# One output group moved across a block boundary, and vector work re-dealt in the second stage of a two-stage block kernel

## The reference

```python
h = layernorm(x) * (1 + ca) + sa
# mixer
qkv = rms(h) @ w_qkv.T;  q, k, v = split(qkv);  q, k = rms(q), rms(k)
w = exp(k)
y = sigmoid(q) * (cumsum(w * v) / (cumsum(w) + 1e-6))      # along the tokens
u, g = split(y @ w_swiglu.T)                                # 2048 each
x = x + ga * (h + (u * silu(g)) @ w_out.T)
# feed-forward, 4-bit weights with a scale for each group of 128 inputs
h = layernorm(x) * (1 + cb) + sb
gate, up = split(h @ dequant(gate_up).T)                    # 1408 each
y = (silu(gate) * up) @ dequant(down).T
x = x + gb * y / rms(y)
```

## Time and profile before

| | us |
|---|---|
| median of three runs | 2029.94 (2029.45 to 2031.5) |
| the profiled execution's own time | 2029.91 |
| its span in the profile | 2027.9 |
| PE busy | 1881.1 (93%) |
| DVE / ACT / POOL busy | 1427.0 / 924.6 / 871.1 |
| first swiglu step starts at | 175.2 |
| feed-forward starts at | 1418.0 |

### The profile page before, as it was taken

How to read it: one execution, slowest core, us unless ns; L and a number is a source line. 1 busy time by engine, 2 the same in 40 slices (tenths; PEclk the granted TensorE clock), 3 DMA queues, 4 the chain that set the end, 5 groups by cost and what they waited for, 6 DMA issues and landing times. The chain is left out here.

```text
span 2027.9 us, 25283 instructions
## 1 busy us (share of the span) xinstructions
PE 1881.1 (93%) x8376; PEld 825.8 (41%) x8376; DVE 1427.0 (70%) x1805; ACT 924.6 (46%) x1421; POOL 871.1 (43%) x616
## 2 busy tenths in 40 slices
PE   4738999999999999999999999999999999999797
PEld 1213444444444444444444444444444343344242
DVE  6997687876877686786787675425657757767756
ACT  4435334424423523533442441221666676676574
POOL 0554324423523432432442331221676766767564
PEclk7869999999999999999999999999999999999999
DMA  7223012112021021010211101203301011101011
GB/s 297 81 79 124 27 39 67 59 39 66 10 83 63 17 83 53 28 61 26 66 59 38 46 22 53 79 16 113 137 22 63 4 60 63 35 28 42 0 42 63
DMA packets 66881, 119.38 MB, mean 59 GB/s; under 512 B 4720, under 2 KB 28272, under 8 KB 65264
## 3 DMA queue, kind: packets, MB, share of 16 engines
q1 hardware_dynamic: 66800, 118.40, 17.2%
HBM read 80.11 MB, written 38.27 MB: 58 GB/s over the span
## 5 line engine op out<-in xcount | busy, mean ns | idle before, releaser
L597 PE MATMUL bank<-Y,wsw 128*128 128x512 f16 x3072 | 682.8, 379 | 0.8 <-DVE late L960 0.8
L597 PEld LDWEIGHTS bank<-Y,wsw 128*128 128x128 f16 x3072 | 300.5, 98 | 365.8 <-issue 4.2
L900 POOL TENSOR_TENSOR late<-late 128x512 f16<-128x512 f32 x128 | 181.5, 1418 | 611.1 <-ACT late L750 610.3
L1772 DVE SCALAR_TENSOR_TENSOR f_A<-bank,gu_s,f_A 128x512 f32<-128x512 f32 x352 | 258.6, 741 | 181.8 <-ACT f_A L1605 174.8
L574 PE MATMUL bank<-late,wout 128*128 128x512 f16 x1536 | 352.4, 379 | 4.3 <-POOL late L900 4.3
L1679 POOL TENSOR_TENSOR f_A<-f_A 128x512 f32<-128x512 f32 x176 | 262.0, 1489 | 167.9 <-DVE f_A L1772 167.9
L1605 ACT ACTIVATE f_A<-bank,gu_s 128x512 f32<-128x512 f32 x352 | 240.4, 686 | 163.4 <-PE bank L1537 141.1
L550 PE MATMUL bank<-H,wqkv 128*128 128x512 f16 x1152 | 261.0, 385 | 41.2 <-DVE H L985 30.9
L1501 PE MATMUL bank<-f_HH,f_down_hi 128*128 128x512 f16 x704 | 266.3, 380 | 11.4 <-POOL f_HH L1691 10.4
L960 DVE TENSOR_TENSOR late<-late,bank 128x512 f32<-128x512 f32 x128 | 87.4, 683 | 252.6 <-PE bank L597 248.9
L574 PEld LDWEIGHTS bank<-late,wout 128*128 128x128 f16 x1536 | 149.7, 98 | 194.3 <-issue 19.7
(11 more groups left out here) (160 smaller groups left out, 2075.7 us busy)
## 6 DMA issues: line engine op xcount, KB each, us to landing
X<-xT SPq DMA_DIRECT2D x15, 1024.0 KB, 5.6
room<-packed SPq DMA_DIRECT2D x48, 176.0 KB, 2.4
h_scratch<-X SPq DMA_DIRECT2D x8, 1024.0 KB, 4.4
f_X<-x_scratch SPq DMA_DIRECT2D x8, 1024.0 KB, 5.4
x_scratch<-X SPq DMA_DIRECT2D x28, 256.0 KB, 2.1
h_scratch<-SQ SPq DMA_DIRECT2D x28, 256.0 KB, 2.2
outT<-f_X SPq DMA_DIRECT2D x7, 1024.0 KB, 4.2
wout<-wmodT SPq DMA_DIRECT2D x1, 4096.0 KB, 14.3
```

The costliest lines, as they stand in the source:

```text
L597: mm = nc.tensor.matmul(out[:], wsw[:, pw, k, col:col + P], Y[:, px, k, :], start=(k == 0 and pw == 0 and px == 0), stop=(k == DT - 1 and ...
L900: nc.gpsimd.tensor_tensor(UG[:, j % 2, 1, :], G, UG[:, j % 2, 0, :], ALU.subtract).then_inc(UG_low, 1)
L1772: nc.vector.scalar_tensor_tensor(a, EV[ev_bank(j, m, steps)][:], gu_s[:, which * I_T + j, g:g + 1], a, ALU.mult, ALU.add).then_inc(by_dve, 1)
```

## The change

In the mixer, `output(b, 15)` of blocks 0 to 5 is taken from the end of the block and put behind group 0 of the `qkv` that follows. `n_squares` and `n_sqrt` each stand one copy later. `s1_split` stands ahead of `high(14)`, and `s1_low` at step 14.

In the feed-forward, two of ACT's takes (step 5, m = 4 and 6) in blocks 1 to 7 are done by DVE (`open_tile`), with a semaphore of their own. `add_y` goes from places 14, 17, 20 to 15, 16, 19. `result` goes from DVE to POOL, at places 31, 35, 39 and 43, behind POOL's `low` and ahead of its `half(j, 1)`. The last block's results in the tail stay on DVE.

```diff
@@ qkv (TensorE)
                         n += 1
+                        if not (isinstance(b, int) and b <= 1) and n == 1:
+                            output(b - 2, FT - 1)
@@ swiglu (TensorE)
-                output(b, FT - 1)
+                if not s1:
+                    output(b, FT - 1)
@@ s2_copies (ScalarE)
-                    if n == DT and not (isinstance(b, int) and b == 1):
+                    if n == DT + 1 and not (isinstance(b, int) and b == 1):
                         n_squares(b - 2)
-                    if n == 2 * DT + 1 and not (isinstance(b, int) and b == 1):
+                    if n == 2 * DT + 2 and not (isinstance(b, int) and b == 1):
                         n_sqrt(b - 2)
@@ iteration (ScalarE)
-                    high(b, j)
                     if s1 and j == 14:
                         s1_split(b + 2)
+                    high(b, j)
@@ iteration (VectorE)
-                        if j == 15:
+                        if j == 14:
                             s1_low(n)
@@ ffn
-        ADD_Y = {14: 0, 17: 1, 20: 2}
+        ADD_Y = {15: 0, 16: 1, 19: 2}
-        RESULT = {35: 0, 36: 1, 38: 2, 39: 3}
+        RESULT = {31: 0, 35: 1, 39: 2, 43: 3}
+        OPENS = [(Y_MEAN // DT, 4), (Y_MEAN // DT, 6)]
@@ beside (GpSimd)
+                if prev and place in RESULT:
+                    result(b - 1, RESULT[place])
@@ iteration (ScalarE)
-                        take(b, j, m, steps)
+                        if not by_vector(b, j, m):
+                            take(b, j, m, steps)
@@ VectorE
+            def open_tile(b, j, m, steps):
+                which, g = m // DT, m % DT
+                dve.wait_ge(group_done, GROUPS * (I_T * b + j) + m + 1)
+                nc.vector.tensor_scalar(A[:, slot(j), 2 * which + g // 2, :], EV[ev_bank(j, m, steps)][:],
+                                        gu_s[:, which * I_T + j, g:g + 1], None, ALU.mult).then_inc(opened_dve, 1)
...
+                        if by_vector(b, j, m - 1):
+                            open_tile(b, j, m - 1, steps)
                         take(b, j, m, steps)
```

More of the change, by code:

```diff
@@ L1355, in ffn @@
         scaled, H_high, H_low = map(sem, ("scaled", "H_high", "H_low"))
-        group_done, by_act, by_dve = map(sem, ("group_done", "by_act", "by_dve"))
+        group_done, by_act, by_dve, opened_dve = map(sem, ("group_done", "by_act", "by_dve", "opened_dve"))
         halves, gate_silu, hid_ready = map(sem, ("halves", "gate_silu", "hid_ready"))
@@ L1399, in ffn, with by_vector, opened @@
         NORM_Y = {30: 0, 31: 1, 32: 2, 34: 3}
-        RESULT = {35: 0, 36: 1, 38: 2, 39: 3}
-        assert RESULT.keys().isdisjoint(NORM_Y.keys())
+        RESULT = {31: 0, 35: 1, 39: 2, 43: 3}
+        OPENS = [(Y_MEAN // DT, 4), (Y_MEAN // DT, 6)]
+        def by_vector(b, j, m):
+            return not first(b) and (j, m) in OPENS
+        def opened(b, j, m):
+            if by_vector(b, j, m):
+                return opened_dve, len(OPENS) * (b - 1) + OPENS.index((j, m)) + 1
+            if first(b):
+                return by_act, DT * j + m // 2 + 1
+            skipped = sum(1 for o in OPENS if o < (j, m))
+            return by_act, (DT * I_T - len(OPENS)) * b + len(OPENS) + DT * j + m // 2 + 1 - skipped
         def now(place, start, step=1):
@@ L1467, in sums_left @@
                 pe.wait_ge(by_dve, DT * (I_T * b + steps.start))
-                pe.wait_ge(by_act, DT * (I_T * b + steps.start))
+                pe.wait_ge(*opened(b, steps.start - 1, GROUPS - 2))
             def mean(b):
@@ L1532, in iteration @@
                             back, k = last
-                            pe.wait_ge((by_act, by_dve)[k % 2], DT * (I_T * b + j - back) + k // 2 + 1)
+                            if k % 2:
+                                pe.wait_ge(by_dve, DT * (I_T * b + j - back) + k // 2 + 1)
+                            elif j < back:
+                                pe.wait_ge(*opened(b - 1, I_T - 1, k))
+                            else:
+                                pe.wait_ge(*opened(b, j - back, k))
                         which, g = m // DT, m % DT
@@ L1553, in _ @@
             pe.wait_ge(by_dve, DT * I_T * NB)
-            pe.wait_ge(by_act, DT * I_T * NB)
+            pe.wait_ge(*opened(NB - 1, I_T - 1, GROUPS - 2))
             for c in range(DT):
@@ L1687, in add_y, with result @@
                 nc.gpsimd.tensor_tensor(RSY[:], RSY[:] if n else SQY[:, 0, :], SQY[:, n + 1, :], ALU.add).then_inc(y_sum, 1)
+            def result(b, c):
+                pool.wait_ge(res_loaded, 16 * (b + 1))
+                pool.wait_ge(y_norm, DT * b + c + 1)
+                nc.gpsimd.tensor_tensor(X[:, c, :], X[:, c, :], Y[:, c, :], ALU.add).then_inc(out_ready, 1)
             def low(b, j):
@@ L1769, in take @@
                 dve.wait_ge(group_done, GROUPS * (I_T * b + j) + m + 1)
-                dve.wait_ge(by_act, DT * (I_T * b + j) + m // 2 + 1)
+                dve.wait_ge(*opened(b, j, m - 1))
                 a = A[:, slot(j), 2 * which + g // 2, :]
@@ L1785, in beside @@
                         work(c)
-                for places, work in ((INVERT_Y, invert_y), (NORM_Y, norm_y), (RESULT, result)):
+                for places, work in ((INVERT_Y, invert_y), (NORM_Y, norm_y)):
                     if prev and place in places:
```

## The result

The changed kernel takes 2010.67 us (median of four runs, 2008.06 to 2010.89), beside 2029.7 for the kernel before on the same chip: a ratio of 0.9902 [0.9885, 0.992], so 19 us faster. The forecast was 2012.3, with a range of 2001 to 2021. The profiled execution took 2010.48, its span is 2008.7, 19.2 shorter than the 2027.9 before.

The account below looks back on a forecast made before the run. PE was taken to bound the kernel, busy 1881.1 of 2027.9 us. Mixer 4.8, ordinary feed-forward blocks 10.2, block 6 3.7 and tail -1.1 sum to 17.6 us, giving 2012.3 from 2029.91; range 2001 to 2021, for 8 in 10.

Parts of the forecast that it names:

- Mixer, the stalls removed: In each mixer block, three PE waits of 0.72, 1.38 and 1.04 us go, 3.14 in all.
- rival 4: Words for `decode_chunk` load late behind the residual's stores, delaying copies PE needs; slower, 2036 at 4 us beyond room; chance 0.04.
- Mixer, what comes back: The DVE chain behind `n_sqrt` makes PE wait in `swiglu`, so each of five loop blocks gains 0.62 us, not 3.14.
- rival 1: The DVE chain behind `n_sqrt` does not bind, so the mixer gives 19.2 us: 1998; chance 0.12.
- The last `qkv`: At the mixer's last `qkv`, the gain is the room `hidden(0)` had before, 1.7 us.
- Ordinary feed-forward blocks: Blocks 1 to 5 and 7: fewer waits for POOL and ACT gain 1.7 us each, 10.2 for six.
- The contention: Feed-forward places 30 to 41: `norm_y` and POOL's results wait for each other, costing 1.25 us instead of 1.05.
- rival 2: POOL's results contend with DVE at all four feed-forward places: 0.7 us a block instead of 1.7, 2020.8; chance 0.14.
- Block 6: Feed-forward block 6: norm's root 2.5 us earlier, plus 1.2 for results leaving the DVE chain: 3.7 us gained.
- rival 3: DVE misses instructions at each of the mixer's four loop jumps, so 12.5 us come back: 2024.8; chance 0.04.
- Tail: At the end, the fourth result ahead of `half(10, 1)` makes the last chain later: -1.1 us.
- the forecast's own bounds: Whole kernel: a mixer gain of 0 to 8 us and ordinary blocks of 1.0 to 2.3 each give 2005 to 2019.

## Why the prediction was right, step by step

**Mixer, the stalls removed: right.** All three went, 3.14 us a block; group 0 found H ready, and PE has no wait inside `qkv` that late words of `decode_chunk` would have caused (rival 4 falls).

**Mixer, what comes back: right in mechanism and size.** Forecast was a gain of 0.62 for each block from a chain behind `n_sqrt` that takes most of the 3.14 back. Measured is a period shorter by 0.47 (164.65 to 164.18, forecast 164.0). The chain's links hold: 9.70 us from the reciprocal to `hidden(0)` (forecast 9.56), and 9.10 to the end of `hidden(1)` where 9.09 was forecast. One link was missing. I let PE reach G of step 1 at its own pace and put the first wait at U(1), on `hidden(0)`. In the trace PE waits 1.77 already at G(1), for `silu(0)`, which on ACT stands behind `n_split` and so behind the same DVE chain. The 0.2 us ahead of `hidden(0)`, which I had read as a wait for PE, is there again with DVE's own reciprocal named for it. The wait at G(1) costs little more, because U(1) comes 2.59 behind G(1) and would have waited for `hidden(0)` anyhow: that G, U pair is 5.54 long instead of 5.35, so both conditions end within 0.2 us of each other. The experiment with the root moved back proves the chain, and refutes rival 1 (nothing comes back).

**The last `qkv`: right.** Forecast was 1.7 for it. PE's second sum for the K norm comes once a block, ahead of the new waits, and marks the blocks: between these marks the intervals were 167.54, four times 164.65 and 165.02, and are 162.90 and five times 164.17. The first gained 4.64, 1.5 more than the three stalls, because waits in block 0's own `swiglu` fell away too (before 0.90 for POOL's sum and 0.53 for its low part). That is not the edit's doing. The kernels with the same mixer as the changed one have these waits in five profiles (0.91 to 1.68, and 0.53), among them the mixer's edits alone, and lack them in one (without `OPENS`, which runs at the lower clock there for a while); their first interval is 164.63 to 165.42, not 162.90. With the mixer of before it was 167.54 and 168.42. So the edit is worth about 3 in the first interval, what the stalls cost, and the rest is scatter between executions. The four gained 0.48 each, the last 0.85, and behind the last mark 1.76 came back. The total, 5.6, is thus 1.5 of scatter, 5 x 0.47, and about 1.8 for the last `qkv`. Without the scatter it is 4.1, and the forecast's 4.8 has 0.7 too much in the five blocks.

**Ordinary feed-forward blocks: right.** 1.85 to 2.06 each, forecast 1.7. The wait of 0.93 went; place 24 waits 0.83 for `low(4)` (forecast 0.8); place 36 costs 0.57 (0.85), and place 34 0.16 (0.4). The contention was over-sized: `norm_y` of place 32 took 1.10 us beside the first result, not 1.76, and that result, which also lay beside the end of `norm_y` of place 31, 1.72 instead of the 1.26 of the others. DVE's two `norm_y`, then POOL's results:

```profile
1596.96 0.98 DVE L1783 SCALAR_TENSOR_TENSOR f_Y<-f_Y,mod,f_RY 128x512 f32<-128x512 f32 x1
...
1598.53 1.10 DVE L1783 SCALAR_TENSOR_TENSOR f_Y<-f_Y,mod,f_RY 128x512 f32<-128x512 f32 x1
```
```profile
1597.36 1.72 POOL L1715 TENSOR_TENSOR f_X<-f_X,f_Y 128x512 f32<-128x512 f32 x1
...
1604.20 1.27 POOL L1715 TENSOR_TENSOR f_X<-f_X,f_Y 128x512 f32<-128x512 f32 x1
```

At the other three places DVE had only takes from a bank, and neither engine was slowed; rival 2 falls. By the three kernels that take a part back, `add_y` is worth 1.1 and `OPENS` 0.7; the results' move is worth 0.1 (69.32 to 69.34 against 69.40 to 69.42, block 1 69.49 against 69.57).

**Block 6: 3.7 forecast, 1.98 measured; the missing term is the clock.** The norm's root comes 1.85 us earlier in the block (49.12 to 47.27 into it), not 2.5. The 1.2 for the results leaving the DVE chain did come. The two waits that I had counted for them, 1.25 at place 38 and 0.40 at place 40 in the kernel before, are gone, and they are back in the two kernels that have the results on DVE, but for the first where a spell covers it. Behind the root's wait the block takes 40.83 before and 40.84 with the results on DVE; with three of them on POOL 39.57, and with all four and `add_y` back 39.17, neither with a spell at the lower clock. That is 1.3 and 1.7 less, with 0.6 paid for contention at place 33 already in it (a wait of 0.93 where it was 0.30). The changed kernel takes 40.70 there, because its spell at place 36 costs 1.5. So 1.85 + 1.66 - 1.53 = 1.98. The kernel before paid nothing for its own spell. My forecast had no term for the clock, though the column in the earlier trace rows said 0.98 for this block.

**The loop's edge at block 4: not in the sum.** I used only to imagine such edges in the mixer (rival 3, which did not come). In the feed-forward the results' move sent the 1 MB load from 0.5 us ahead of the jump to 6.4 behind it, worth 2.15 beyond the ordinary gain. With the 1.7 in block 6, which the spell hid, it is what the results' move brought: ordinary blocks would have had their gain without it.

**Tail: wrong in size, -1.1 forecast.** The fourth result delays `half(10, 1)` as I put it, by about 0.9 us of wait. In this execution the longer wait was followed by the lower clock, which added 1.7:

```profile
1987.93 0.38 PE L1518 MATMUL bank<-f_HH,f_down_hi 128*128 128x512 f16 x1 [2.39 <-POOL f_HH L1719]
...
1989.43 1.06 PE L1518 MATMUL bank<-f_HH,f_down_hi 128*128 128x512 f16 x2
```

From the last down projection's first matmul to the norm's sum are 5.21 us, before 3.53. With the fourth result on DVE the wait is 1.46 and the pair takes 0.59:

```profile
1987.70 0.38 PE L1519 MATMUL bank<-f_HH,f_down_hi 128*128 128x512 f16 x1 [1.46 <-POOL f_HH L1720]
1988.13 0.59 PE L1519 MATMUL bank<-f_HH,f_down_hi 128*128 128x512 f16 x2
```

So -2.6 instead of -1.1, of which -0.9 is the mechanism that I had forecast and -1.7 the clock. The kernel with `n_lower` later has the changed kernel's feed-forward and the same wait of 2.39, and no spell: 3.53 us from there to the norm's sum, and block 7 with the tail takes 94.3 instead of 96.0, 1.2 less than before where I had forecast 0.6 less.

The total came within 1.6 us because the misses cancel, and that is luck: mixer +0.8, ordinary blocks and block 7 +1.4, prologue +0.4, loop's edge +2.2, against -1.7 in block 6 and -1.5 in the tail. The plus of the mixer comes from the scatter of its first block, and the 0.44 of the prologue is scatter too: over the thirteen profiles the first `swiglu` step starts between 172.3 and 175.2, in kernels that do not differ there. Both big minuses are spells at the lower clock. The range that I gave for the forecast's own bounds, 2005 to 2019, was also too narrow by its own terms: a mixer of 0 with ordinary blocks of 1.0 makes 2021.

**Do the spells come in every execution?** Four kernels share the changed kernel's feed-forward: itself, the feed-forward's edits alone, the root one copy earlier, and `n_lower` later. In block 6 all four have the spell at the same place (87.97 to 87.99). In the tail three have it and one has not. The three kernels with three results on POOL share a feed-forward as well, and have no spell, one and two in block 6 (86.50, 86.46 and 87.61). So the same instructions and the same waits come with and without it, and it moves a single time by 1 to 2 us. What decides it stays open. Open too is which instructions come late at the jump, and for which engine.

## What to carry to other kernels

When stalls are removed ahead of a chain on another engine, ask when that chain's head is due on the new clock: here the head was moved one step later to cure a stall of 1.04 us, and the chain behind it cost 2.74. Follow every queue that hangs on the chain, not only the engine at its end: ACT's `silu` stood behind a split that waited for the same tiles. When work is moved between engines, follow the DMAs that its completion releases, and where they land against a loop's jump. And before a stretch of one trace is compared with another's, look at its granted clock: a spell hid 1.5 us of gain in block 6 here and cost nothing in the kernel it was compared with.

## What the runs showed of the hardware

- **A hardware loop's jump.** After the jump of the feed-forward loop DVE stood idle 2.7 to 3.3 us in ten kernels, and 5.2 to 5.4 in the three where a 1 MB load was issued 0.5 us ahead of the block's start. The block was then 3.3 us longer than an ordinary one (5.0 where the lower clock followed) instead of 0.8 to 1.4. Issued 0.25 us behind the start the load cost nothing that shows. In the block's first 3 us the queue for instructions carried one or two packets in the dear cases and three in the cheap ones.
- **The clock after a wait.** In the tail a wait of 2.39 us was followed by 1.2 GHz in four of six profiles, one of 1.5 in none of seven. In block 6 a wait of 2.62 at place 36 was followed by it in seven of thirteen. At the loop's jump a wait of 2.52 was followed by it and one of 2.97, in the kernel before, was not. So which waits bring it down could not be told from their length alone. A spell cost 1.5 to 1.7 us where PE's own pace set the time, and nothing where PE had to wait for another engine afterwards.
- **Two engines on one memory.** A `norm_y` on DVE takes 0.73 alone, and took 1.10 beside a POOL add, which took 1.72 instead of 1.26; takes from a bank ran beside POOL's adds at their usual length. The Trainium skill (SBUF — State Buffer, "Who interferes with whom") has such instructions exclude each other on a shared port; the trace agrees, in that both grew, `norm_y` by 0.37 and the add, which lay beside two of them, by 0.46.
